# A decoder layer on one core: weight loads moved to one queue in another order, each engine's loop entered at its own iteration, and all engine orders and PSUM banks chosen anew

## The reference, cut to what matters

```python
x = layernorm(x + attn(x))        # random-feature attention, 16 heads of 16, 64 features a head
x = layernorm(x + xattn(ctx, x))  # softmax cross attention, 16 heads, keys and values from ctx
x = layernorm(x + ffn(x))         # gate/up/down, 256 -> 1024 -> 256

# attn: q,k,v = x@W.T+b ; phi(y) = exp(orf.y/2 - |y|^2/8) + eps ; (phi_q (phi_k^T v)) / (phi_q sum phi_k) ; @Wo.T+bo
# xattn: softmax((q Wq)(ctx Wk)^T / 4) (ctx Wv)
# ffn: ternary weights (w / mean|w| rounded and clipped to -1..1), activations rounded to 127 levels;
#      silu(gate) * up, again rounded, then down
```

## Time and profile before

| | us |
|---|---|
| median of 3 runs | 508.16 |
| lowest, highest | 504.93, 509.95 |
| the profiled execution, its own time | 505.92 |
| its span (first to last instruction) | 504.2 |

### The profile page before, as it was taken

One profiled execution on the slowest core, in us unless ns is written; L12 is line 12 of the kernel. 1 busy time (PEld: TensorE's weight loads), 2 busy tenths in 40 slices (PEclk: granted clock), 3 DMA queues, 4 the chain that ended last, 5 costly groups with the idle time before them and its releaser, 6 DMA issues.

```text
span 504.2 us, 18524 instructions
## 1 busy us (share of the span) xinstructions
PE 438.9 (87%) x6566; PEld 304.7 (60%) x6566; DVE 450.6 (89%) x1355; ACT 428.8 (85%) x908; POOL 365.5 (72%) x789
## 2 busy tenths in 40 slices
PE   4568888998999998999999999999999999876641
PEld 2235666666776766776767676777676766543310
DVE  4667686999999999899999999999999999999771
ACT  2247789999999998999999999999999999867532
POOL 1447767778788888788888888888888876763422
PEclk9979899999999999999999999999999999999875
DMA  7665566787768787566666666666666687542212
GB/s 186 230 125 101 133 116 109 107 154 124 127 130 134 157 140 133 133 146 146 146 146 141 140 139 135 144 140 142 136 145 136 137 139 127 85 75 62 55 33 63
DMA packets 192659, 64.27 MB, mean 127 GB/s; under 512 B 172384, under 2 KB 192352, under 8 KB 192608
## 3 DMA queue, kind: packets, MB, share of 16 engines
q1 hardware_dynamic: 190080, 60.46, 60.4%
q10 hardware_dynamic: 2528, 3.15, 1.7%
HBM read 17.31 MB, written 4.19 MB: 43 GB/s over the span
## 4 chain that ended last, share of the span: by engine, by line
PE 58%; ACT 13%; DMA 11%; DVE 7%; issue 5%; SPq 3%; POOL 3%; ACTq 0%; POOLq 0%; DVEq 0%
PE bank L1131 10%; PE bank L1335 9%; DMA tT<-pkT 4%; PE bank L1306 4%; PE bank L1225 4%; PE bank L1362 4%; PE bank L1183 3%; DMA ffn_ld<-in_L_ffn_w_down_dram 3%; PE bank L1204 2%; PE bank L1145 2%; PE bank L1240 2%; PE bank L1322 2%; PE bank L1150 2%; PE bank L1211 2%; PE bank L1294 2%
## 5 line engine op out<-in xcount | busy, mean ns | idle before, releaser
L1131 PE MATMUL bank<-wq_hi,xT 128*128 128x512 f16 (+1 forms) x256 | 72.5, 338 | 3.7 <-DVE vv L816 2.3
L434 POOL TENSOR_TENSOR ve<-mv,lneps 128x1 f32<-128x1 f32 x96 | 19.4, 202 | 63.4 <-DVE mv L866 48.0
L438 POOL TENSOR_TENSOR rs<-ve,mhalf 128x1 f32<-128x1 f32 x96 | 55.0, 573 | 0.0
L946 DVE SCALAR_TENSOR_TENSOR g<-th,bank 128x512 f32<-128x512 f32 x64 | 43.4, 678 | 4.7 <-ACT th L653 4.3
L558 ACT ACTIVATE x<-y,nmr,rs 128x256 f32<-128x256 f32 x64 | 39.8, 622 | 7.9 <-DVE y L1007 4.4
L630 ACT ACTIVATE pT<-bank 128x512 f32<-128x512 f32 x64 | 37.8, 591 | 9.7 <-PE bank L1296 8.1
L897 DVE TENSOR_REDUCE negm<-bank 128x4 f16<-128x512 f32 x64 | 43.4, 678 | 1.6 <-PE bank L1260 1.2
L898 DVE TENSOR_REDUCE negm<-bank 128x4 f16<-128x512 f32 x64 | 43.5, 680 | 0.0
L577 ACT ACTIVATE phk<-bank 128x512 f32<-128x512 f32 x64 | 39.4, 617 | 4.5 <-PE bank L1150 4.5
L1131 PE MATMUL bank<-wq_lo,xT 128*128 128x256 f16 (+1 forms) x128 | 43.2, 337 | 0.0
L425 POOL TENSOR_TENSOR pkA<-qk,pkA 128x512 f16<-128x512 f32 x32 | 37.6, 1175 | 7.0 <-ACT pkA L520 6.6
(11 more groups left out here) (184 smaller groups left out, 1580.0 us busy)
## 6 DMA issues: line engine op xcount, KB each, us to landing
xs<-in_x_dram SPq DMA_DIRECT2D x32, 128.0 KB, 2.3
cs<-in_ctx_dram SPq DMA_DIRECT2D x32, 128.0 KB, 2.3
xr<-in_x_dram SPq DMA_DIRECT2D x32, 128.0 KB, 2.3
out_dram<-ot SPq DMA_DIRECT2D x32, 128.0 KB, 1.8
ffn_ld<-in_L_ffn_w_gate_dram ACTq DMA_DIRECT2D x1, 1024.0 KB, 9.0
ffn_ld<-in_L_ffn_w_up_dram ACTq DMA_DIRECT2D x1, 1024.0 KB, 11.5
ffn_ld<-in_L_ffn_w_down_dram ACTq DMA_DIRECT2D x1, 1024.0 KB, 13.8
pkAT<-pkA SPq DMA_TRANSPOSE x64, 3.2
```

Source lines behind the costliest of these rows:

```text
L438: g.tensor_tensor(rs[n - 1][:, :], ve[n - 1][:, :], mhalf[:, :], ALU.pow).then_inc(done[f"pw{n}"], 1)
L946: v.scalar_tensor_tensor(g1[:, n, :], th[:, n, :], 1.0, gate, ALU.add, ALU.mult).then_inc(done[f"gl{n}"], 1)
L1131: last = T.matmul(o, xT[:, 2 * part + c, :], w[:, c, cols], start=(n == 0), stop=(n == 5))
```

## The change

**Loads.** SP issues everything large: x of tile 0, Wq, Wk, Wv, x of tile 1, gate, up, the three biases, down, then Wo and its bias. ACT issues only the four small loads. POOL waits for the bias of Wo in the step that uses it (`xb_`), not ahead of the first x.

**One-time work.** On DVE all three `magnitudes` and `ffn_scales` stand ahead of the iterations, and the nine passes stand in iterations 0 to 5. On PE `ffn_means` and the transposes of Wo stand ahead of the first `xTp`.

**Loop entry.** `run` takes the number of draining iterations and the first looped iteration from each engine:

| engine | drains, first looped before | now |
|---|---|---|
| SP | 13, 16 | 14, 14 |
| POOL | 13, 16 | 12, 14 |
| ACT | 13, 16 | 11, 14 |
| DVE | 13, 16 | 9, 10 |
| PE | 13, 16 | 9, 10 |

**Orders and banks.** Every `iteration` has its steps in a new order, some with another lag, and nearly all PSUM names have another bank. With the banks, the waits that guard them changed. Three semaphores (`xb`, `sd`, `bs1`) are gone, one (`s1`) is new. No step of a tile was added or removed.

```diff
-        def run(eng, iteration, lags=LAGS, first=FIRST):
+        def run(eng, iteration, lags, first):
...
         @block.sync
         def _(sp):
+            load_first(0)
             for n, w in enumerate((Wq, Wk, Wv)):
                 sp.dma_start(wld[:, n, :, :], w.rearrange("(o p) i -> p o i", p=P)).then_inc(w_in[n], 16)
+            load_first(1)
...
+            load_ffn()
             late_weights()
+            load_down()
...
-            run(sp, iteration)
+            run(sp, iteration, 14, 14)
...
         def _(pool):
-                pool.wait_ge(bo_in, 16)
...
         def _(act):
-            load_ffn()
-            load_down()
             evacuate_wo()
...
         def _(dve):
             clear_packs()
+            magnitudes[0]()
+            magnitudes[1]()
+            magnitudes[2]()
             feature_weights()
-            magnitudes[0]()
+            ffn_scales()
...
         def _(pe):
             output_weight()
+            ffn_means()
...
             def iteration(i, par):
+                go(phk0, i, par, 3)
+                go(phk1, i, par, 3)
+                go(tm, i, par, 6)
...
-            run(pe, iteration)
+            run(pe, iteration, 9, 10)
```

More of the change, by code:

```diff
@@ L561, in x1_ @@
             def x1_(t, par):
+                wait(act, "rs1", t)
                 wait(act, "ya2", t, -2)
@@ L1057, in iteration @@
                 go(bs2, i, par, 6)
-                once(scales_of[0], i, 2)
-                go(gl0, i, par, 7)
+                go(hu0, i, par, 7)
+                once(scales_of[0], i, 0)
                 go(y2, i, par, 6)
-                once(clear_values, i, 4)
-                go(gl1, i, par, 7)
-                go(hu0, i, par, 7)
                 go(hu1, i, par, 7)
-                go(tlo, i, par, 4)
-            run(dve, iteration)
+                go(hh0, i, par, 7)
+                once(scales_of[2], i, 4)
@@ L1069, in _ @@
+                go(ad3, i, par, 8)
+                once(clips_of[1], i, 2)
+                go(nr, i, par, 0)
+                go(tlo, i, par, 4)
+                go(ad1, i, par, 3)
+                go(hh1, i, par, 7)
+                go(bs1, i, par, 3)
+                go(hx, i, par, 7)
+                once(clips_of[2], i, 5)
+                go(am, i, par, 6)
+            run(dve, iteration, 9, 10)
         @block.tensor
@@ L1222, in wo @@
                 first_time(pe, t, 0, prep_ev, 4)
-                wait(pe, "tlo", t, -1)
+                wait(pe, "kvm", t, 1)
                 for k in range(2):
@@ L1229, in x1Tp @@
                 wait(pe, "x1", t)
-                wait(pe, "v", t, 4)
+                wait(pe, "gl0", t, -3)
                 for k in range(2):
@@ L1237, in tm @@
                 wait(pe, "x1T", t)
-                wait(pe, "gl0", t, -3)
                 for k in range(2):
@@ L1254, in s0 @@
             def s0(t, par):
+                first_time(pe, t, 0, ffn_out, 3)
                 wait_moved(pe, "tT", t, par)
-                wait(pe, "ad1", t, 1)
-                wait(pe, "ephk1", t, 3)
                 for k in range(4):
@@ L1270, in s1 @@
                                     start=True, stop=True)
-                last
+                last.then_inc(done["s1"], 1)
             def mTp(t, par):
-                wait(pe, "m1", t)
+                wait(pe, "aT", t, 2)
                 T.transpose(at_mT.bitcast(F16), negm[:, :, :].rearrange("p e h -> p (e h)"),
@@ L1278, in st0 @@
             def st0(t, par):
-                wait(pe, "kvm", t, 3)
-                wait(pe, "xT", t, 6)
+                wait(pe, "ad1", t, 2)
+                wait(pe, "ephk1", t, 4)
                 for k in range(4):
@@ L1315, in pv1 @@
                 wait(pe, "p1", t)
-                wait(pe, "ad3", t, -3)
                 weigh(1, par, "pv1")
@@ L1320, in oxp @@
                 wait(pe, "oxT", t)
+                wait(pe, "at", t, 3)
                 for q in range(4):
@@ L1365, in _ @@
             output_weight()
+            ffn_means()
             def iteration(i, par):
-                if isinstance(i, int) and i == 6:
-                    pe.wait_ge(ffn_out, 2)
-                once(ternaries[2], i, 6)
-                go(phk1, i, par, 3)
+                go(phk0, i, par, 3)
+                go(phk1, i, par, 3)
+                go(tm, i, par, 6)
+                if isinstance(i, int) and i == 3:
+                    pe.wait_ge(done["v"], 2)
+                once(ternaries[1], i, 3)
+                go(wo, i, par, 5)
+                go(nump, i, par, 4)
+                go(st1, i, par, 7)
+                go(st0, i, par, 7)
+                go(qkm, i, par, 1)
+                if isinstance(i, int) and i == 2:
+                    pe.wait_ge(scales, 5)
+                once(ternaries[0], i, 2)
+                if isinstance(i, int) and i == 6:
+                    pe.wait_ge(done["ad1"], 2)
+                once(ternaries[3], i, 6)
+                if isinstance(i, int) and i == 9:
+                    pe.wait_ge(done["nT"], 6)
+                once(ternaries[5], i, 9)
                 go(ntp, i, par, 4)
-                if isinstance(i, int) and i == 6:
-                    pe.wait_ge(done["vh"], 1)
-                once(ternaries[3], i, 6)
-                go(phk0, i, par, 3)
                 go(pv1, i, par, 7)
@@ L1380, in iteration @@
                 go(s1, i, par, 6)
-                go(qkm, i, par, 1)
+                go(phq1, i, par, 3)
                 go(xqTp, i, par, 8)
                 go(oxp, i, par, 7)
-                go(phq1, i, par, 3)
                 go(phq0, i, par, 3)
-                if isinstance(i, int) and i == 7:
-                    pe.wait_ge(done["vh"], 2)
-                once(ternaries[4], i, 7)
-                go(vm, i, par, 1)
-                go(kvs, i, par, 3)
                 go(g0, i, par, 8)
```

305 lines of the change are left out of this document (146 added, 159 removed), and 8 rows, old and new, of the table done.

## The result

| | before | now | ratio, 95% interval |
|---|---|---|---|
| median, us (14 runs each, same chip) | 507.22 | 512.05 | 1.0093 (1.0066 to 1.0121) |
| again, on another chip (10 and 12 runs) | 507.65 | 511.39 | 1.0076 (1.0043 to 1.0108), to all 32 runs of before there |
| profiled execution, its span | 505.92, 504.2 | 511.71, 510.0 | |

The change made the kernel slower by 0.8 to 0.9%, 4 to 5 us. The forecast was 504.4 in a range of 496 to 512, 0.7% faster. Of the rivals the second (the late start is kept, about 513) came nearest.

A forecast was written before the change was run, and what follows sets the result against it. Three full engines (DVE, ACT, PE) and an equally tight ring through tT's DMA bound the loop; the ring alone decides the fill. Terms +5.0 − 2.0 − 4.4 − 2.4 − 1.0 + 1.0 = −3.8 gave 504.4 us, range 496 to 512.

The forecast's parts named there:

- Part 1: Loads and start: first qk 7.2 us late, some regained by kvT of tile 0; net +5.0 us, bounds +1 and +7.2.
- I take 2.2 of these 4.97 as regained: Start: of DVE's 2.68 us standing for down and 2.29 summing it, 2.2 us won back by kvT of tile 0.
- Part 2: Iterations 2 to 5: most of DVE's ternary passes now done earlier in idle time; −2.0 us, bounds 0 and −5.
- Part 3: Iterations 5 to 8, the fill: each of four periods shrinks by 1.1 us; −4.4 us, bounds 0 and −7.
- the ring: Chain from s0 to tm (PE), tlo (DVE), transposing DMA for tT, next s0; 12.96 us, the whole loop period.
- Part 5: The loop: 12.97 rather than 13.01 us a tile over 23 tiles; −1.0 us, bounds −3 and +4.
- Part 4: Loop entered earlier: tiles 10 to 16 at 13.01 rather than 13.41 us each; −2.4 us, bounds 0 and −3.5.
- its mark: Sign for the earlier loop entry: q8's instruction fetches end near iteration 10, tiles 10 to 16 take 13.0 us each.
- The rival of a stall at each branch: Loop: each of PE's 11 turns stands for 1 us, +11 us, giving 515 us; chance 0.04.
- Part 6: Drain: hh1 now stands behind ad3 in the serial chain for the last two or so tiles; +1.0 us, bounds −1 and +2.
- rival 2: Start: nothing of the 7.2 us won back, early iterations bound by pkA's two transposes; +4.8 or more, 513 us; chance 0.12.

The follow-up runs named there:

- e8: Changed kernel without rounding and clipping of the three feed-forward weights (six DVE passes left out): 509.23 us, ratio 1.0030 to the kernel before.
- e17: e9 with ACT taking thi ahead of hi in unrolled iterations: 507.41 us, ratio 1.0017 to the kernel before.
- e18: e12's kernel with ACT taking thi ahead of hi in unrolled iterations: 509.28 us, ratio 1.0047 to the kernel before.
- e5: Changed kernel, but in iterations 0 to 13 SP issues kT directly behind tT, ahead of two loads and cT: 533.19 us, ratio 1.0467 to before.
- e9: e12's kernel with SP issuing cT directly behind tT, ahead of the loads, in unrolled iterations: 503.03 us, ratio 0.9907 to the kernel before.
- e10: e9 with POOL also taking ya2 ahead of chi and xb in unrolled iterations: 508.04 us, ratio 0.9997 to the kernel before.
- e13: e9 with the last ternary transposes (PE) and last copy of downT (ACT) one iteration earlier: 503.10 us, ratio 0.9915 to the kernel before.
- e2: Changed kernel with every engine entering its loop at iteration 16, as before: 515.82 us, ratio 1.0207 to the kernel before.
- e11: e12's kernel with every engine entering its loop at iteration 16: 512.02 us, ratio 1.0058 to the kernel before.
- e12: Changed kernel with Wo loaded behind Wv, first x ahead of the wsum product, down summed behind tile 0's qk and v: 504.18 us, ratio 0.9923 to before.

## Why the prediction missed

**Part 1** failed in its last step. The qk of tile 0 was foreseen at 26 and came at 25.3; down landed at 18.4, near the 19 assumed. The step that failed is "I take 2.2 of these 4.97 as regained". Nothing was: from the first qk to kvT of tile 0 it was 16.7 us before and 17.3 now. The prediction counted one ternary pass there. The timeline of DVE has five, 7.1 us (the others at 30.57, 32.31 and 33.55), where the kernel before had none. They were to fill idle time, but some stand in front of steps that the first tile needs.

```profile
26.93 1.64 DVE L799 TENSOR_SCALAR ffn_t<-ffn_ld,wscale 128x2048 f32<-128x2048 f32 x1
28.93 1.12 DVE L841 CAST pkA<-nrm 128x32 f16<-128x32 f32 x1
...
41.29 1.44 DVE L804 TENSOR_SCALAR ffn_ld<-ffn_t 128x2048 f32<-128x2048 f32 x1
42.66 0.41 DVE L855 TENSOR_TENSOR kvT<-bank,vsum 128x256 f32<-128x256 f32 x1
```

e8 measures them: without six passes, three of them in this stretch (3.9 us), kvT of tile 0 is 2.7 us earlier, about what was to be regained (two traces of one kernel differ by up to 1.3 there). The prediction's own terms also give 7.4 to 7.5 for the late qk, not 7.2. The upper bound of +7.2 was passed in both pairs of traces, by 0.1 and by 1.7.

**Part 2** (−2.0) measured −0.9 to −1.3, right in kind.

**Part 3** failed outright: −4.4 became +1.7 and more from kvT 3 to 7. The step that failed is "qkm no longer lies on the ring", taken as a saving of 1.40 us a period with nothing put in its place. From before, PE's tm and s0 and DVE's tlo between them, in the stretch of 85 to 99 us:

```profile
85.61 0.23 PE L1259 MATMUL bank<-cT,tT 64*128 64x128 f16 x1 [0.20 <-DMA tT<-pkT]
...
92.48 0.61 PE L1240 MATMUL bank<-gblk,x1T 128*128 128x128 f32 x4
...
98.23 0.21 PE L1259 MATMUL bank<-cT,tT 64*128 64x128 f16 x1
```

```profile
93.76 0.42 DVE L891 TENSOR_TENSOR pkT<-bank,pkT 128x256 f16<-128x256 f32 x1
```

And the same steps now (PE, then ACT and DVE between tm and s0):

```profile
92.52 0.23 PE L1265 MATMUL bank<-cT,tT 64*128 64x128 f16 x1
...
97.77 0.35 PE L1257 MATMUL bank<-wvp,cT 128*128 128x32 f16 x8
...
98.67 0.61 PE L1161 MATMUL bank<-orfp,pkAT 128*128 128x128 f16 x8
99.13 0.71 PE L1248 MATMUL bank<-gblk,x1T 128*128 128x128 f32 x4
...
106.03 0.23 PE L1265 MATMUL bank<-cT,tT 64*128 64x128 f16 x1 [0.70 <-DMA tT<-pkT]
```

```profile
99.22 1.08 ACT L531 ACTIVATE pkA<-qk 128x1024 f16<-128x1024 f32 x1
100.16 0.62 ACT L531 ACTIVATE pkT<-bank 128x512 f16<-128x512 f32 x1
```

```profile
100.82 0.42 DVE L899 TENSOR_TENSOR pkT<-bank,pkT 128x256 f16<-128x256 f32 x1 [0.26 <-ACT pkT L531]
```

Before: s0 to tm 6.87, tm to tlo 1.28, tlo to s0 4.47, in all 12.62. Now: 6.61, 1.69, 5.21, in all 13.51. Instead of 1.40 the way from s0 to tm lost 0.26, ACT's hi came between tm and tlo (+0.4), and tT lands 0.7 later. PE works through the way from s0 to tm in both kernels, so its length is that of the list. qkm is gone from it, but vhp (97.77, 0.20 to the next start) and phk (98.67, 0.46) are new in it, and small gaps take most of the rest. Part 5 of the same prediction says that they are "of about the same length" as what they replace; Part 3 left them out. That is the arithmetic of one period. That hi's place alone causes the later tlo and the longer period is not shown: with hi out of the way (e17, e18) the fill grew longer. e5 shows a second ring, through cT, chi, ya2 and x1, and in the changed kernel POOL stood 7.6 us in four waits for cT between 60 and 112. e9, e10, e13, e17 and e18 each relax one of the rings and none shortens the fill by more than about 1 us; which of them binds in each period stays open.

**Part 4** (−2.4) measured −2.3 and −2.5, and its mark is there: q8 fetched once between 130 and 208 us, instead of ten times, and tT landed after 3.1 us. What I did not see is that the new order needs the early entry: without it, it loses 3.1 (e2) and 5.5 us (e11) on the same six tiles. The bound of 3.5 holds only for the old order. The rival of a stall at each branch did not come: the loop is as fast as before. The Trainium skill ("Runtime: NRT & Kernel Launch", instruction fetch mechanics) prefers full unrolling, because a taken branch to a target outside the instruction window forces a fetch. It says nothing against a loop whose code lies inside the window, so the prediction's "By it, a loop turn would cost a stall" reads too much into it, and the single fetch in the loop does not contradict it. As advice to unroll this kernel, e11 beside e12 disagrees: four tiles took 57.1 us with the entry at 16 and 52.1 with the early entry.

**Part 5** (−1.0) measured −0.1 to −0.4, inside its bounds; no engine gained from DVE's new slack, since PE (194.69 of 194.9) and ACT took its place. Its list of what is exchanged missed dn, which now stands ahead of tm: from s0 to tm the loop takes 309.50 − 301.99 = 7.51 us and not 7.15, and tlo to s0 314.98 − 310.83 = 4.15 in place of 4.48, the sooner landing of tT that Part 5 thought possible. That the two nearly cancel, and the ring stayed at 12.99, is luck. **Part 6** (+1.0) measured +0.5 to +1.2, though hh1 was not shown to be the cause: the chain of waits goes, from 421.9 to 438.5, through hqT, dn, tm, tlo and cT to x1.

With Part 1 at +7.3 and Part 3 at +1.4 in place of +5.0 and −4.4, the same sum gives 7.3 − 2.0 + 1.4 − 2.4 − 1.0 + 1.0 = +4.3: slower, near what was measured. I gave rival 2, which says nearly this, 0.12. Its condition (down later than 20 us) was not even needed; two waits in a row on PE, each for the last loads, were enough. Its other half, that the two transposes of pkA bind the early iterations, is not shown by any run.

## What to carry to other kernels

Put nothing that waits for the last loads ahead of the first useful instruction on an in-order engine, and look for every such wait: here two ended within 2 us, and removing one gave nothing. In a pipeline whose loop is full, a late start is paid nearly in full at the end (6.8 us at tile 0, 5.8 at tile 28), since little behind it runs faster to win it back. When a step leaves a ring, list what takes its place there before counting it as saved. The time at which a queue issues something is not the time at which it was ready: before moving an item up in a serial queue, find out what it waits for, or all that stands behind it will wait too.
